# Output weights' operands made beside the query projections and kept in DRAM, and a unit's last two transposes in the outputs' bank

## The reference

```python
xn = _layernorm(x)
qkv = xn @ w_qkv                                  # 1024 x (32 + 8 + 8) * 128
scores = einsum('bqhgd,bkhd->bhgqk', q, k) * scale
attn = softmax(scores + bias)                     # bias = -slope * sqrt(i - j), -inf for j > i
out = einsum('bhgqk,bkhd->bqhgd', attn, v) @ w_o  # w_o: 4096 x 1024
x = x + out + (xn @ W.T + b + lora of the routed rank)
```

## Time and profile before

| | us |
|---|---|
| median of 3 runs | 2472.9 (2472.09 to 2473.75) |
| the profiled execution | 2475.28 |
| its span | 2473.4 |
| granted clock of TensorE, mean | 0.991 of full speed |
| TensorE busy | 96% |
| VectorE, ScalarE, GpSimd busy | 63%, 56%, 32% |
| moved by DMA | 455.90 MB, 184 GB/s over the span |

### The profile page before, as it was taken

The page is one execution under the profiler, slowest core; times in us unless marked ns, Lnnn a source line. Parts: engine busy times, 40 slices in busy tenths (PEclk is TensorE's granted clock), DMA queues, the critical chain, the costliest instruction groups (busy, mean ns, idle before and its releaser), DMA issues.

```text
span 2473.4 us, 34303 instructions
## 1 busy us (share of the span) xinstructions
PE 2377.9 (96%) x11616; PEld 1991.7 (81%) x11616; DVE 1547.1 (63%) x2969; ACT 1373.4 (56%) x3051; POOL 784.2 (32%) x1029
## 2 busy tenths in 40 slices
PE   5999999998799999999899999999999999999999
PEld 4787888887678788888778888788888888888887
DVE  5657355655655645555676666767667666676665
ACT  4532133334533223333477777777777777777774
POOL 3211000000330100000244645446455464554644
PEclk9999999999899999999999999999999999999999
DMA  4536445546254635445655565655655556666553
GB/s 151 182 129 209 146 146 184 191 170 236 71 175 157 207 120 204 153 170 196 235 185 182 188 230 203 208 194 188 226 201 210 198 188 218 201 211 206 187 175 141
DMA packets 118318, 455.90 MB, mean 184 GB/s; under 512 B 11945, under 2 KB 12089, under 8 KB 109184
## 3 DMA queue, kind: packets, MB, share of 16 engines
q1 hardware_dynamic: 86176, 334.37, 39.2%
q0 software_dynamic: 31968, 119.33, 13.9%
HBM read 276.96 MB, written 176.69 MB: 183 GB/s over the span
## 4 chain that ended last, share of the span: by engine, by line
PE 85%; DVE 5%; ACT 4%; issue 3%; DMA 3%; POOL 1%; SPq 0%; ACTq 0%; DVEq 0%; POOLq 0%
PE ps L677 26%; PE ps L678 26%; PE ps L679 26%; PE ps L877 5%; DMA lora_lo<-lora_s 1%; DMA qk_s<-res_b 1%; ACT probs L1085 1%; ACT res_hi L945 1%; DVE stats L1197 1%; DVE wo L1183 1%; ACT rows L974 1%; PE ps L857 1%; ACT probs L1107 1%; DVE w_lo L1183 0%; DMA qk_s<-res_hi 0%
## 5 line engine op out<-in xcount | busy, mean ns | idle before, releaser
L945 ACT ACTIVATE w_hi<-raw 128x1024 fp32r<-128x1024 f32 x196 | 207.0, 1059 | 558.9 <-PE ps L679 439.5
L1467 DVE TENSOR_TENSOR acc<-ps,acc 128x512 f32<-128x512 f32 x448 | 297.2, 686 | 287.3 <-issue 260.8
L1183 DVE TENSOR_TENSOR w_lo<-raw,w_hi 128x1024 fp32r<-128x1024 f32 x196 | 239.1, 1224 | 357.8 <-ACT w_hi L945 357.6
L677 PE MATMUL ps<-x_hi,w_hi 128*128 128x512 f32 x1120 | 436.5, 390 | 0.0
L678 PE MATMUL ps<-x_lo,w_hi 128*128 128x512 f32 x1120 | 436.0, 389 | 0.0
L679 PE MATMUL ps<-x_hi,w_lo 128*128 128x512 f32 x1120 | 435.9, 389 | 0.0
L1085 ACT ACTIVATE probs<-probs,neg_max 128x512 f32<-128x512 f32 (+3 forms) x512 | 283.9, 566 | 168.8 <-DVE neg_max L1432 168.8
L677 PE MATMUL ps<-wo,op_hi 128*128 128x512 f32 x896 | 363.5, 406 | 2.0 <-POOL op_lo L635 0.7
L678 PE MATMUL ps<-wo,op_hi 128*128 128x512 f32 x896 | 352.1, 393 | 0.0
L679 PE MATMUL ps<-wo,op_lo 128*128 128x512 f32 x896 | 351.5, 392 | 0.0
L679 PEld LDWEIGHTS ps<-x_hi,w_lo 128*128 128x128 f32 x1120 | 210.4, 188 | 43.9
(11 more groups left out here) (166 smaller groups left out, 4637.1 us busy)
## 6 DMA issues: line engine op xcount, KB each, us to landing
raw<-w_all SPq DMA_DIRECT2D x70, 1024.0 KB, 5.4
q<-qk_s SPq DMA_DIRECT2D x128, 512.0 KB, 3.9
acc<-acc_s SPq DMA_DIRECT2D x128, 512.0 KB, 5.1
acc_s<-acc SPq DMA_DIRECT2D x112, 512.0 KB, 7.7
qk_s<-res_hi POOLq DMA_DIRECT2D x40, 1024.0 KB, 4.6
qk_s<-res_a POOLq DMA_DIRECT2D x20, 1024.0 KB, 9.2
qk_s<-res_b POOLq DMA_DIRECT2D x20, 1024.0 KB, 5.2
k<-qk_s SPq DMA_DIRECT2D x32, 512.0 KB, 3.6
```

The costliest lines, as they stand in the source:

```text
L677: pe.matmul(to, st_hi, mv_hi, start=start, stop=False, skip_group_check=True)
L945: nc.scalar.activation(to, source, ACT.Copy).then_inc(signal, 1)
L1183: nc.vector.tensor_tensor(to, source, high.bitcast(F32), ALU.subtract).then_inc(signal, 1)
L1467: nc.vector.tensor_tensor(to, fill[f % 2][:, :], to, ALU.add).then_inc(s_acc, 1)
```

## The change

The splits and sums of the output weights leave the attention. The weights are cut into 32 quarters (four of 256 columns for each of 8 groups), seven operands each: 224 jobs (JOBS) of 128x256, 112 in each pair, done beside the steps of Q0 to Q3 by STEP_JOBS and LAST_JOBS (30 in each of Q0 to Q2, 22 in Q3). A job is a high on ScalarE and a low on VectorE into one of four slots (SLOTS) of `wp`, and a store of 262 KB (runs of 1 KB) by SyncE to `wo_s` in DRAM; the high of job j waits for the store of job j - 4. A quarter's four raw blocks (131 KB each) are loaded by SyncE, and its four sums made by VectorE, in place, after its third job. The first half of a step's jobs stands ahead of `weights(n + 1, 1)`, the second at the step's end; the stores stand between the loads of `raw` in SyncE's order.

In the attention SyncE loads each finished operand as 1 MB: group 0's at n = 1 (four) and n = 2 (three), later ones' steps 0 to 3 in the turns 10 to 13 of the group before and steps 4 to 6 in turn 6 of their own group; there are 11 places for nine, and TensorE's fills wait for the loads (s_wo). The last two transposes go to ps_o, the outputs' bank, and the waits for ps_c on TensorE go. Other edits are of the layout only (bias and wo at other addresses).

```diff
-WO_SUMS_IN = {6: (4, 2), 7: (5,), 8: (3,)}
-HIGHS_IN = {6: (1,), 7: (2,), 8: (0, 6), 9: (3, 4), 10: (5,)}
-LOWS_EARLY = {9: (2,), 10: (4,)}
-LOWS_LAST = {6: (1,), 8: (0, 6), 9: (3,), 10: (5,)}
-WO_PLACES = 9
+WO_ORDER = (6, 1, 0, 4, 2, 5, 3)
+STEP_JOBS = (3, 5, 4, 5, 5, 4, 4)
+LAST_JOBS = (3, 5, 4, 5, 4, 2, 0)
+SLOTS = 4
+WO_PLACES = 11
...
-        t_banks = [(ps_t0, 0, 512), (ps_t1, 512, 512), (ps_c, 1024, 256)]
+        t_banks = [(ps_t0, 0, 512), (ps_t1, 512, 512), (ps_o, 1024, 256)]
...
+                for j in jobs(pr, m, st, part_):
+                    c, i = j // STEPS, j % STEPS
+                    part = slice(c % 4 * 256, (c % 4 + 1) * 256)
+                    sp.wait_ge(s_wp_lo, j + 1)
+                    sp.dma_start(wo_s[c // 4, WO_ORDER[i], :, :, part], wp[:, j % SLOTS].bitcast(F32)
+                                 ).then_inc(s_wp_out[j % SLOTS], 16)
+                    if i >= 3 and (c + 1) % (QUARTERS // PAIRS):
+                        sp.wait_ge(s_wp_sum, 4 * (c + 1))
+                        quarter(c + 1, {3: 2, 4: 3, 5: 1, 6: 0}[i])
...
             def out_weights(n):
 
                 if n in (1, 2):
-                    sp.wait_ge(s_bank, 4 * TOTAL)
-                    for i in ((0, 2), (1, 3))[n - 1]:
-                        out_block(0, i)
-                group = n // GROUP_UNITS
-                if n % GROUP_UNITS == 2 * G + 2 and group + 1 < GROUPS:
-                    sp.wait_ge(s_wo_lo, STEPS * (group + 1))
-                    sp.wait_ge(s_wo_sum, len(WO_SUMS) * (group + 1))
-                    for i in range(4):
-                        out_block(group + 1, i)
+                    if n == 1:
+                        sp.wait_ge(s_bank, 4 * TOTAL)
+                        operands_are_out(JOBS)
+                    for step in (range(0, 4), range(4, STEPS))[n - 1]:
+                        out_operand(0, step)
+                group, since = n // GROUP_UNITS, n % GROUP_UNITS
+                if since == 6 and group:
+                    for step in range(4, STEPS):
+                        out_operand(group, step)
+                if since in range(10, 14) and group + 1 < GROUPS:
+                    out_operand(group + 1, since - 10)
...
-                    if n >= 2 and i == 3:
-                        pe.wait_ge(s_pt_lo, 3 * (n - 1))
...
-                    if to is ps_c and n + 1 < UNITS:
-                        pe.wait_ge(s_neg_max, QT * (n + 1) + 1)
...
-                    pe.wait_ge(s_wo_lo, low_made(s // (SETS // GROUPS), k))
+                    pe.wait_ge(s_wo[k], 16 * (s // (SETS // GROUPS) + 1))
...
+            def job(j):
+
+                c, step = j // STEPS, WO_ORDER[j % STEPS]
+                if j >= SLOTS:
+                    act.wait_ge(s_wp_out[j % SLOTS], 16 * (j // SLOTS))
+                if step in (0, 1, 6):
+                    act.wait_ge(s_wp_raw[{0: 0, 1: 1, 6: 3}[step]], 16 * (c + 1))
                 else:
-                    i = {0: 0, 1: 1, 6: 3}[step]
-                    act.wait_ge(s_wo_raw[i], 16 * (group + 1))
-                high(wo[:, wo_place(group, step), 0], wo_source(group, step), s_wo_hi)
+                    act.wait_ge(s_wp_sum, 4 * c + (4, 2, 5, 3).index(step) + 1)
+                high(wp[:, j % SLOTS, 0], wp_source(step), s_wp_hi)
...
                         later_operand(pr, m, st, 1)
+                        for j in jobs(pr, m, st, 0):
+                            job(j)
                         weights(n + 1, 1)
                         gate_parts(pr, m, st)
                         ahead(pr, m, st)
+                        for j in jobs(pr, m, st, 1):
+                            job(j)
...
+                low(wp[:, j % SLOTS, 1], wp_source(WO_ORDER[i]), wp[:, j % SLOTS, 0], s_wp_lo)
+                if i != 2:
+                    return
+                a11, a12, a21, a22 = (r[:, :] for r in wp_raw)
+                dve.wait_ge(s_wp_raw[2], 16 * (c + 1))
+                nc.vector.tensor_tensor(a21, a11, a21, ALU.subtract).then_inc(s_wp_sum, 1)
+                dve.wait_ge(s_wp_lo, j + 1)
+                dve.wait_ge(s_wp_sum, 4 * c + 1)
+                nc.vector.tensor_tensor(a22, a22, a21, ALU.subtract).then_inc(s_wp_sum, 1)
```

More of the change, by code:

```diff
@@ L353, in op_used, with jobs, wp_source @@
             return PARTS * s + part - STEPS + 1
[L357 to L371, removed]
+        def jobs(pr, m, st, part=None):
+            if m not in QUERIES:
+                return []
+            first, count = 0, 0
+            for m_ in range(Q0, m + 1):
+                for st_ in range(STEPS if m_ < m else st + 1):
+                    first += count
+                    count = (LAST_JOBS if m_ == LAST else STEP_JOBS)[st_]
+            per_pair = JOBS // PAIRS
+            mine = [pr * per_pair + j for j in range(first, min(first + count, per_pair))]
+            half = (len(mine) + 1) // 2
+            return mine if part is None else mine[:half] if part == 0 else mine[half:]
+        def wp_source(step):
+            return wp_raw[{0: 0, 1: 1, 6: 3, 4: 2, 2: 3, 5: 1, 3: 0}[step]][:, :]
         def wo_place(group, step):
[L374 removed]
+            return (STEPS * group + step) % WO_PLACES
         def used(group, step):
[L378 removed]
+            turn_ = STEPS * group + step - WO_PLACES
             if turn_ < 0:
[L380 removed]
+                return None
             last = SETS // GROUPS * (turn_ // STEPS + 1) - 1
[L382 to L387 removed]
+            return PARTS * last + STEPS + turn_ % STEPS + 1
         block = ctx.enter_context(nc.Block())
@@ L669, in _ @@
                     out_low(s, part)
-                for group, step in making(n, WO_SUMS_IN):
-                    wo_sums(group, step)
         @block.tensor
@@ L1169, in _ @@
                     normalise(n)
-                for part in making(n, HIGHS_IN):
-                    out_split(*part)
         @block.vector
@@ L1520, in _ @@
                     add_fill(*f)
-                for part in making(n, LOWS_LAST):
-                    out_split(*part)
 def constants():
```

109 lines of the change are left out of this document (54 added, 55 removed).

## The result

The changed kernel takes 2561.9 us (2561.15 to 2562.38) where the kernel before takes 2472.6 beside it: 1.036 times as long, 95% interval 1.0342 to 1.0378. It is 89 us slower and 108 us above the forecast. The range ended at 2467, so the time lies outside it, on the side to which I gave a chance of 0.07.

The account below looks back on a forecast made before the run. TensorE, busy 96% of the span, was taken as the bound. Attention boundaries -28.9, attention start +4, matrix starts +4 and pair's transition +2 sum to -18.9: 2472.9 to 2454.0 us, range 2444 to 2467.

Parts of the forecast that it names:

- Part 1: Attention: no output weights made there and third transposes wait for no maximum, so waits at seven boundaries go, -28.9 us.
- Part 2: Start of the attention: q loads land late behind the output weights' operands, +4 us, from -1 to +9.
- the upper end of my own range (+9): Start of the attention: q(2)'s whole delay of 10 to 12 us less 3, +9.
- Part 3: Jobs beside the query projections: 0 in mid-matrix, +4 us where matrices change, +2 at the pair's transition.
- Its terms for the work: Query projections: highs and lows take 413 and 412 ns, hidden mid-matrix; three jobs at the pair's transition cost 1.05 us.
- Its term for the queue: Query projections: each job of 0.337 MB takes about 1 us of DMA queue.
- the new wait: Query projections: ScalarE waits for a slot's store of four jobs before; not met with stores landing inside 8 us.
- The cover that I named: Query projections: idle time before w_lo, 357.8 us in all, ahead of which ScalarE waits for TensorE, hides mid-matrix jobs, cost 0.
- Rival D: Query projections: the DMA queue becomes the bound, at 248 GB/s +28 us, about 2482 us; chance 0.08.
- Its sign to tell: Query projections: TensorE gaps in every step, with a DMA share near 1.00 over whole matrices.
- rival B: Every cover holds: matrix starts cost 0, the pair's transition 1, the attention's start -1; about 2444 us; chance 0.20.

Follow-up runs that it names:

- the two runs on the bank: Kernel before with third transposes in ps_o and without the ps_c waits, 2481.4 us; changed kernel with its last two transposes back in ps_c, 2561.9 us.
- the late loads: Changed kernel with group 0's seven operands loaded two at a time in turns 4 to 7, not in turns 1 and 2: 2553.8 us.

## Why the prediction was wrong

**Part 1, -28.9: right.** From the 17th unit to the last the gain is 29.3. L873, once a unit:

```profile
L873 PE MATMUL ps<-k,q x98: 222/223/223, 1455.6 to 2370.1; 128*128 128x128 f32 x98
```

97 units in 914.5 us: 48 pairs of 18.90 and one of 7.03 are 914.2. No boundary is left, and the loads of 7.3 MB a group cost nothing (DMA share 0.70; +35 GB/s on 203 were forecast, 246 in all were measured). But the reason was half right. I let the wait of L877 carry the cost; the two runs on the bank show that the wait was only where the delay was met, and that the bank brings nothing.

**Part 2, +4: the mechanism right, the size half.** The first 16 units took 8.6 us more in the changed kernel, 7.4 without jobs. TensorE waited 11.24 us for q(2), for 3.13, and went on 27.0 us behind the start of the first unit for 15.0: 12 later, where 10 to 12 were forecast. For q(4) it waited only 1.18, for 3.90:

```profile
1316.84 1.97 SPq L488 DMA_DIRECT2D wo<-wo_s  x4
1318.85 0.44 SPq L553 DMA_DIRECT2D q<-qk_s  x1
```

```profile
1335.06 0.80 PE L693 MATMUL ps<-k,q 128*128 128x512 f32 x1 [11.24 <-DMA q<-qk_s]
...
1346.27 0.50 PE L693 MATMUL ps<-k,q 128*128 128x512 f32 x1 [1.18 <-DMA q<-qk_s]
```

I took the delay of the last q, 7 us, less 3. It is that of the first late one, 12 us, less the 3.4 that came back, which was the upper end of my own range (+9).

**Part 3, +6 for the jobs: the step that failed**, 107.4 measured at the start of the first unit. Its terms for the work held: a high took 416 ns and a low 420, for 413 and 412 by the like forms, and the hand work in all +2.1 (about 5 by the traces), 0.96 of it at the transition for 1.05. Its term for the queue held too. In Q1 the DMA engines were taken 0.74 x 94.5 = 69.9 us, less 0.51 x 76.1 = 38.8 of before, 31.1 for 30 jobs: 1.04 us each, for "about 1 us". What failed is the sentence that with stores landing inside 8 us the new wait is not met, and the wait for the blocks, for which there is no sentence at all: both stood at nothing in the sum. Nine in ten stores did land inside 8 us of their issue (the longest took 12.4); what the sentence left out is the time up to the issue, the jobs in a row and the blocks. Alone the slots cost 41 us over the hand work and the blocks 16, together 105. Both are loops through DRAM, and I had most of the numbers for them. A job comes every 76.2 / 30 = 2.54 us; a block returns after three jobs, 7.6 us, a slot after four, 10.2, and after less when up to three jobs stand in a row in one half of a step. Against that stand SyncE's own turns (0.7 to 1.5 us for each issue in the rows of the chain, and the wait for the last low of a bunch) and the landing, 5.8 us for a block and 5.2 for a store in the median, 9.8 for one behind a 1 MB load. The kernel before had landings of that size in view, 5.4 us for a 1 MB load and 9.2 for res_a (KB each, median us to landing):

```profile
raw<-w_all SPq DMA_DIRECT2D x70, 1024.0 KB, 5.4
...
qk_s<-res_a POOLq DMA_DIRECT2D x20, 1024.0 KB, 9.2
```

I had asked whether the queue could carry the bytes, not when one transfer comes back to its buffer.

The cover that I named, the time in which ScalarE waits for TensorE ahead of w_hi, was there, and half of it was used up (before, then after; the number behind <-PE is that time in us, over the whole span):

```profile
L945 ACT ACTIVATE w_hi<-raw 128x1024 fp32r<-128x1024 f32 x196 | 207.0, 1059 | 558.9 <-PE ps L679 439.5
...
L957 ACT ACTIVATE w_hi<-raw 128x1024 fp32r<-128x1024 f32 x196 | 205.8, 1053 | 339.8 <-PE ps L695 225.3
```

It did not cover the single waits: they are up to 7.5 us long, and the slack ahead of a w_hi was 4.4 by my own reading at the start of a matrix.

**Rival D** had the sign and not the cause as it was stated. It put the decision at 1.24 us of queue a job; the jobs took 1.04 and the queue was never full over a matrix, 0.70 to 0.80, and yet 107 us went. Its sign to tell, a share near 1.00 over whole matrices, did not appear. What did appear is a full queue in bursts (0.97 in the chain of 12 us, 0.20 in the stretch from 404 to 408 below), which lengthens the landing and so the loops. The fit from the Trainium skill ("DMA: Bandwidth & Descriptors", "Anatomy of one DMA"), given there for a DMA that GpSimd issues, makes an estimate of 2.6 us for a store of 262 KB. A store landed here in 5.2 us from SyncE and in 6.5 from GpSimd, and took 1.04 us of the engines' time with its share of the reloads, so the estimate was too low as a landing time and too high as a price one after the other. That the covers hold, as rival B had it, was true for the work alone.

## What to carry to other kernels

A buffer that goes through DRAM and back is a loop: the number of buffers times the time between two uses must exceed the turn of the issuing queue, the time behind the bulk transfers, and the landing (here 7.6 us against 12), for the densest bunch and not for the mean. A queue with a quarter of its time free doesn't show this; ask of each wait when the buffer was freed and how many uses lie between. And before work is moved out of a stage, look for a gap of its engine within the stage: three lows in another place gave 22.7 us, where the move of all the work would at best have given about 27 (18.7 without any job, and 8.1 from the late loads, if the two add up).

## What the runs showed of the hardware that I had not expected

Short waits cost TensorE more than their length. After the 3.33 us wait that ends at 408.16 in the changed kernel the granted clock fell, here four windows (PEclk is the third number from the end):

```profile
404.00:408.00 4.00, 0.83 (x4) 0.37 (x2) 3.15 (x3) 2.21 (x4) 0.00 (x0) 1.00 0.20 64
409.00:413.00 4.00, 4.00 (x12) 3.18 (x11) 3.45 (x5) 1.77 (x4) 0.00 (x0) 0.59 0.26 85
409.70:413.10 3.40, 3.40 (x10) 2.66 (x9) 2.75 (x5) 1.11 (x2) 0.00 (x0) 0.50 0.33 106
414.00:420.00 6.00, 6.00 (x28) 4.95 (x27) 2.76 (x7) 1.79 (x3) 0.00 (x0) 1.00 0.94 253
```

Between 404 and 408 TensorE had been busy 0.83 us. From 409.7 to 413.1 the granted clock is 0.50, the lower of the clock's two levels (1.2 for 2.4 GHz), and a matmul starts every 0.43 us in place of 0.23; then the clock is back. Over Q1 the same matmuls are busy 82.49 us for 76.10, so of the 18.4 us that Q1 lost, 12.0 are waits and 6.4 longer matmuls. The mean granted clock of Q1 is 0.95, and the 0.05 that is missing of 94.5 us explains about 5 of the 6.4; the rest is not traced. The whole stretch from Q0 to the first unit shows the same, 76 us more of waits (99.2 for 23.7) and 33 more of busy time; below are Q1 of the kernel before, then the stretch before and after.

```profile
377.90:454.00 76.10, 76.10 (x337) 63.04 (x336) 42.31 (x37) 27.94 (x33) 6.03 (x8) 1.00 0.51 179
...
301.70:1200.60 898.90, 875.24 (x3865) 721.14 (x3864) 508.24 (x518) 324.86 (x387) 100.26 (x124) 0.99 0.48 168
...
300.50:1308.00 1007.50, 908.29 (x3865) 733.45 (x3864) 634.99 (x870) 398.11 (x611) 101.16 (x125) 0.96 0.67 224
```

What stays open: with the stores on GpSimd and four jobs of distance 62 us are still lost. Half the bytes halve this, so about half of it goes with what stands in the queues, and the cause of the other half is open. How much more slots would bring, and what the same bytes would cost without any wait for them, was not tried.
